# Per-image mixed 3x3 convolution on one core: pair 0's first weights summed on TensorE, pair 1's root on GpSimd, and loads from pair 8 on issued after the stores have landed

## What is computed

```python
pooled = x.mean(axis=(2, 3))                       # x: group-normalised input, 32 x 64 x 56 x 56, 32 groups
a = relu(pooled @ fc1_w.T + fc1_b)                 # K = 4 values per image
att = softmax(a @ fc2_w.T + fc2_b, axis=1)         # four mixing weights per image
agg_w = einsum('bk,koihw->boihw', att, weight)     # each image has its own 3x3 kernel
agg_b = att @ bias
out = x_raw + conv3x3(x, agg_w, pad 1) + agg_b     # x_raw: the input before the normalisation
```

## Time and profile before

| | us |
|---|---|
| median of 3 runs (304.75 to 305.0) | 304.8 |
| the profiled execution | 304.24 |
| its span, first to last instruction | 302.5 |
| TensorE busy | 297.2 (98% of the span) |
| VectorE, ScalarE, GpSimd busy | 245.9, 189.7, 17.7 |
| first product of pair 0 | 13.82 |
| granted TensorE clock, mean | 1.00 |

### The profile page before, as it was taken

How to read it: one execution, slowest core, us unless ns; L and a number is a source line. 1 busy time by engine, 2 the same in 40 slices (tenths; PEclk the granted TensorE clock), 3 DMA queues, 4 the chain that set the end, 5 groups by cost and what they waited for, 6 DMA issues and landing times.

```text
span 302.5 us, 15876 instructions
## 1 busy us (share of the span) xinstructions
PE 297.2 (98%) x7065; PEld 273.1 (90%) x7065; DVE 245.9 (81%) x799; ACT 189.7 (63%) x246; POOL 17.7 (6%) x30
## 2 busy tenths in 40 slices
PE   8999999999999999999999999999999999999995
PEld 6778997799978997799999999999999999999874
DVE  4898989989999999898998989699696978956000
ACT  3757739194674927385496868577585866768222
POOL 2231040403100000000000000000000000000000
PEclk9999999999999999999999999999999999999999
DMA  7857866647457583846708788765657242332333
GB/s 268 317 168 214 262 184 200 215 146 191 152 163 218 175 243 135 223 144 173 258 14 245 239 242 266 204 197 165 191 150 240 95 123 70 111 102 81 93 113 104
DMA packets 27012, 53.62 MB, mean 177 GB/s; under 512 B 6080, under 2 KB 16704, under 8 KB 26944
## 3 DMA queue, kind: packets, MB, share of 16 engines
q1 hardware_dynamic: 26720, 52.53, 57.6%
q10 hardware_dynamic: 224, 0.07, 0.1%
HBM read 26.89 MB, written 25.69 MB: 174 GB/s over the span
## 4 chain that ended last, share of the span: by engine, by line
PE 95%; DMA 3%; ACT 0%; POOL 0%; DVE 0%; issue 0%; DVEq 0%
PE acc L1068 94%; DMA w_sb<-w_t 1%; DMA x<-x 1%; ACT o L875 0%; PE acc L1048 0%; PE acc L1036 0%; PE tiny L1005 0%; POOL wnorms L418 0%; DVE o L792 0%; PE tiny L1022 0%; PE tiny L1026 0%; PE acc L1042 0%; DVEq L790 0%
## 5 line engine op out<-in xcount | busy, mean ns | idle before, releaser
L1068 PE MATMUL acc<-xh,wh 64*64 64x385 f16 (+5 forms) x2304 | 112.6, 325 | 0.0
L1068 PE MATMUL acc<-xh,wl 64*64 64x385 f16 (+5 forms) x2304 | 112.4, 325 | 0.0
L1068 PE MATMUL acc<-xl,wh 64*64 64x385 f16 (+5 forms) x2304 | 111.7, 325 | 0.0
L1068 PEld LDWEIGHTS acc<-xl,wh 64*64 64x64 f16 x2304 | 91.3, 107 | 6.0
L1068 PEld LDWEIGHTS acc<-xh,wl 64*64 64x64 f16 x2304 | 90.6, 107 | 6.8
L1068 PEld LDWEIGHTS acc<-xh,wh 64*64 64x64 f16 x2304 | 89.5, 107 | 7.2 <-ACT wh L864 0.3
L914 ACT ACTIVATE o<-acc,par 128x392 f32<-128x392 f32 (+1 forms) x64 | 42.9, 671 | 56.9 <-PE acc L1068 56.9
L458 DVE BATCH_NORM_STATS2 stats<-x 128x6 f32<-128x448 f32 x105 | 61.2, 617 | 1.8
L835 ACT ACTIVATE xh<-x,xof,xsc 128x1568 f16<-128x1568 f32 x24 | 40.5, 1689 | 25.1 <-DVE xof L545 24.6
L702 DVE TENSOR_TENSOR xl<-x,xh 128x1568 f16<-128x1568 f32 x28 | 49.8, 1783 | 3.3 <-ACT x L802 3.2
L593 DVE SCALAR_TENSOR_TENSOR mix<-w_sb,ex,mix 128x576 f32<-128x576 f32 (+1 forms) x69 | 42.8, 620 | 0.5
(11 more groups left out here) (106 smaller groups left out, 161.6 us busy)
## 6 DMA issues: line engine op xcount, KB each, us to landing
x<-x SPq DMA_DIRECT2D x60, 392.0 KB, 4.0
out<-o SPq DMA_DIRECT2D x36, 196.0 KB, 3.6
out<-o SPq DMA_DIRECT2D x72, 98.0 KB, 2.8
out<-o SPq DMA_DIRECT2D x8, 588.0 KB, 3.3
out<-o SPq DMA_DIRECT2D x16, 294.0 KB, 4.2
w_sb<-w_t SPq DMA_DIRECT2D x2, 576.0 KB, 4.1
x<-x SPq DMA_DIRECT2D x2, 448.0 KB, 4.2
out<-o SPq DMA_DIRECT2D x7, 112.0 KB, 2.2
```

The costliest lines, as they stand in the source:

```text
L1068: ins = nc.tensor.matmul(pixels[:, top:bottom, left:right], weights[i][halves[m], tap * C:(tap + 1) * C], window, start=start and step == ...
```

## The change

1. **Start of pair 0, TensorE.** All four shares of the three centre-row taps are summed on TensorE: the centre tap (64 columns) in `acc[2][1]` with the residual, the two side taps (128 columns) in `tiny[0]`. `part_mix` and VectorE's addition are gone. ScalarE reads both sums from PSUM (`first_high_weights`), and so does VectorE for the low part. The products begin with the centre tap of all three groups, then the side taps of all three, and then go on as before. `keep_warm` has 2 products after the range instead of 4, 3 and 3. The second product of the weights' norm is moved ahead of the semaphore `s_range`.
2. **Start of pair 0, VectorE and ScalarE.** VectorE makes four `diagonals`, then `wsc`, then two strips of xh that ScalarE made before (3 and 6); ScalarE has strip 7 alone left, later. `low_inputs(0, 0)` comes before the weights' bound and before all seven chunks of pair 1's statistics.
3. **Pair 1's root.** `second_group_stats` takes the root from GpSimd (`ALU.pow`), behind `second_low_inputs(0)` on its queue, in place of the Newton steps. The sums of pair 1 are asked for 2 steps into group 2's last kind and not 6; the first chunk of pair 2 moves behind the logits of pair 1.
4. **Pairs 8 to 11, SP.** Before each quarter of x, SP waits until the stores of this group have landed.

The core of the diff:

```diff
-WARM_PRODUCTS = (38, 6, 15, 4, 3, 3)
+WARM_PRODUCTS = (38, 6, 15, 2)
...
-SUMS_AT = ((1, 2, 6), (1, 2, 2), (1, 2, 2), (1, 1, 8), (1, 0, 8), (1, 0, 1), (0, 2, 6), (0, 2, 4), (1, 0, 2))
+SUMS_AT = ((1, 2, 2), (1, 2, 2), (1, 2, 2), (1, 1, 8), (1, 0, 8), (1, 0, 1), (0, 2, 6), (0, 2, 4), (1, 0, 2))
...
+        def first_piece(n, t):
+
+            return (t[:, CENTRE * C:(CENTRE + 1) * C], sides(t), t[:, PARTS[1]], t[:, PARTS[2]])[n]
+
+        def mixed_piece(n):
+
+            if n == 0:
+                return acc[SLOTS - 1][1][:, CENTRE_SUM]
+            if n == 1:
+                return tiny[0][:, SIDES_SUM].rearrange("p (t c) -> p t c", c=C)
+            return mix[:, PARTS[n - 1]]
...
                         cross_params(p + 1)
                     if p + X_RING < PAIRS:
+
+                        for r in range(2):
+                            sp.wait_ge(stored[p % 2][r], 16 * (1 + r) * (transfers(p) + g + 1))
                         load_quarter(p + X_RING, g)
...
+            second_low_inputs(0)
+            pool.wait_ge(s_mv, 2)
+            nc.gpsimd.tensor_tensor(rstd[:], mv[:, 1:2], minus_half[:], ALU.pow).then_inc(s_root, 1)
+            for p in range(1, EARLY):
                 second_low_inputs(p)
...
+                for k in range(K):
                     nc.vector.tensor_scalar(diagonals[:, k, :], eye[:], ex[:, k:k + 1], None, ALU.mult).then_inc(s_diagonal, 1)
+                    if k == 0:
+                        nc.vector.tensor_reduce(exsum[:], ex[:], AX.X, ALU.add).then_inc(s_exsum, 1)
+                for k in range(2):
+                    first_scale_step(k)
+                high_strip(6)
+                high_strip(3)
+                low_part(0)
+                dve.wait_ge(s_weights[0], 16)
...
             high_strip(4)
             first_mixture()
+            dve.wait_ge(s_scaled, 1)
+            low_inputs(0, 0)
             weights_bound()
             chunk_stats(1, 0, 1)
-            dve.wait_ge(s_scaled, 1)
-            low_inputs(0, 0)
             chunk_stats(1, 1, CHUNKS)
             exchange_stats(1)
-            group_stats(1)
+            second_group_stats()
             for p in range(1, EARLY):
                 logits(p)
+                if p == 1:
+
+                    chunk_stats(2, 0, 1)
                 mixture_in_parts(p)
...
             exponentials(0)
 
             first_high(5, 6, s_quarter[2])
-            first_high(2, 4, s_quarter[1])
-            high_weights_part(0, 0)
-            first_high(6, 8, s_quarter[3])
+            first_high(2, 3, s_quarter[1])
+            first_high_weights(0)
+            first_high_weights(1)
             first_share(2)
             first_high(0, 1, s_quarter[0])
-            high_weights_part(0, 1)
+            first_high_weights(2)
+            act.wait_ge(s_v_strip, 3)
+            first_high(7, 8, s_quarter[3])
 
             normalise_quarter(0, 1)
-            high_weights_part(0, 2)
+            first_high_weights(3)
             normalise_quarter(0, 2)
             normalise_quarter(0, 3)
...
+            def centre_share(k):
+
+                pe.wait_ge(s_weights[k // 2], 16)
+                pe.wait_ge(s_diagonal, k + 1)
+                for m in range(2):
+                    nc.tensor.matmul(acc[SLOTS - 1][1][halves[m], CENTRE_SUM], diagonals[halves[m], k, :],
+                                     first_piece(0, w_sb[:, k, :])[halves[m]], start=k == 0, stop=False)
+
+            def sides_share(k):
+
+                for m in range(2):
+                    ins = nc.tensor.matmul(tiny[0][halves[m], SIDES_SUM].rearrange("p (t c) -> p t c", c=C),
+                                           diagonals[halves[m], k, :], first_piece(1, w_sb[:, k, :])[halves[m]],
+                                           start=k == 0, stop=k == K - 1)
+                    if k == K - 1:
+                        ins.then_inc(s_sides_sum, 1)
+
+            def first_residual():
+
                 pe.wait_ge(s_eye, 1)
                 pe.wait_ge(s_eye_exsum, 1)
-                centre = slice(PART_SUM.start + C, PART_SUM.start + 2 * C)
                 for m in range(2):
-                    nc.tensor.matmul(acc[SLOTS - 1][1][halves[m], centre], eye_exsum[halves[m], :], eye_std[halves[m], :],
-                                     start=False, stop=True).then_inc(s_part_sum, 1)
+                    nc.tensor.matmul(acc[SLOTS - 1][1][halves[m], CENTRE_SUM], eye_exsum[halves[m], :],
+                                     eye_std[halves[m], :], start=False, stop=True).then_inc(s_centre_sum, 1)
...
             keep_warm(3)
-            part_sum()
-            weights_range()
-            keep_warm(4)
-
-            pe.wait_ge(s_part, 2)
-            keep_warm(5)
-
-
-            for n in range(len(PARTS)):
-                steps = range(3 * n, 3 * n + 3)
+
+            centre_share(0)
+            sides_share(0)
+            centre_share(1)
+            centre_share(2)
+            centre_share(3)
+            first_residual()
+            for k in range(1, K):
+                sides_share(k)
+
+
+
+            for n in range(2):
                 pe.wait_ge(s_wh, n + 1)
                 for g in range(SLOTS):
```

More of the change, by code:

```diff
@@ L422, in _ @@
             nc.gpsimd.tensor_scalar(eye_exsum[:], eye[:], exsum[:], None, ALU.mult).then_inc(s_eye_exsum, 1)
-            for p in range(EARLY):
+            second_low_inputs(0)
+            pool.wait_ge(s_mv, 2)
+            nc.gpsimd.tensor_tensor(rstd[:], mv[:, 1:2], minus_half[:], ALU.pow).then_inc(s_root, 1)
+            for p in range(1, EARLY):
                 second_low_inputs(p)
@@ L863, in high_weights_part, with first_high_weights @@
                 part = PARTS[n]
-                nc.scalar.activation(wh[i][:, part], mix[:, part], ACT.Copy, scale=wsc[i][:]).then_inc(s_wh, 1)
+                nc.scalar.activation(wh[i][:, part], mixed_part(p, n), ACT.Copy, scale=wsc[i][:]).then_inc(s_wh, 1)
+            def first_high_weights(n):
+                if n == 0:
+                    act.wait_ge(s_wsc, 1)
+                    act.wait_ge(s_centre_sum, 2)
+                elif n == 1:
+                    act.wait_ge(s_sides_sum, 2)
+                else:
+                    act.wait_ge(s_part, shares(0, n))
+                nc.scalar.activation(first_piece(n, wh[0]), mixed_piece(n), ACT.Copy, scale=wsc[0][:]).then_inc(s_wh, 1)
             def first_share(n):
@@ L1021, in first_range @@
                 pe.wait_ge(s_wnorms, 1)
-                nc.tensor.matmul(tiny[1][:, RANGE:RANGE + 1], scale[:], wnorms[:], start=False, stop=True).then_inc(s_range, 1)
-            def weights_range():
-                nc.tensor.matmul(tiny[0][:, WEIGHTS:WEIGHTS + 1], scale[:], wnorms[:],
-                                 start=True, stop=True).then_inc(s_weights_range, 1)
-            def part_sum():
-                part = PARTS[0]
-                pe.wait_ge(s_weights[0], 16)
-                for k in range(SUMMED_SHARES):
-                    pe.wait_ge(s_diagonal, k + 1)
-                    for m in range(2):
-                        nc.tensor.matmul(acc[SLOTS - 1][1][halves[m], PART_SUM], diagonals[halves[m], k, :], w_sb[halves[m], k, part],
-                                         start=k == 0, stop=False)
+                nc.tensor.matmul(tiny[1][:, RANGE:RANGE + 1], scale[:], wnorms[:], start=False, stop=True)
@@ new lines, in first_range @@
+                nc.tensor.matmul(tiny[1][:, WEIGHTS:WEIGHTS + 1], scale[:], wnorms[:],
+                                 start=True, stop=True).then_inc(s_range, 1)
+            def centre_share(k):
[4 more added lines that the diff above has]
+                                     first_piece(0, w_sb[:, k, :])[halves[m]], start=k == 0, stop=False)
@@ L1121, in _ @@
                     elif (n, g) == (0, 2):
-                        pe.wait_ge(s_quarter[3], 1)
-                    elif (n, g) == (1, 0):
-                        pe.wait_ge(s_quarter[0], 1)
-                    high(0, g, steps)
-                pe.wait_ge(s_wl, n + 1)
+                        pe.wait_ge(s_v_strip, 3)
+                        pe.wait_ge(s_wl, 1)
+                    high(0, g, (range(1), range(1, 3))[n])
+            for n in range(len(PARTS)):
+                steps = range(3 * n, 3 * n + 3)
+                if n > 0:
+                    pe.wait_ge(s_wh, n + 2)
+                    pe.wait_ge(*((s_quarter[0], 1) if n == 1 else (s_quarter[3], 1)))
+                    for g in range(SLOTS):
+                        high(0, g, steps)
+                pe.wait_ge(s_wl, n + 2)
                 for g in range(SLOTS):
```

83 lines of the change are left out of this document (47 added, 36 removed).

## The result

The changed kernel takes 315.99 us (median of 4 runs, 315.59 to 318.62) against 304.77 for the kernel before beside it (4 runs, 304.42 to 305.0): ratio 1.0389, 95% interval 1.0365 to 1.0413. It is 11.2 us slower; 3.5 were forecast. The four executions took 315.59, 315.64, 316.33 and 318.62 us at mean granted clocks of 0.998, 0.999, 0.995 and 0.988, so the two longer ones lost something to the clock as well. The profiled execution took 315.59, its span 313.8, against 304.24 and 302.5.

A forecast was written before the change was run, and what follows sets the result against it. TensorE's products bound the kernel, 94% of the chain: a 13.8 us start, 16 periods of 17.82 and an end. Profiled 304.24 - 0.3 (start) + 3.8 (SP's waits) = 307.7, median 0.56 above: 308.3 us, range 304.2 to 312.9.

The forecast's parts named there:

- The copy of pair 9: SP's queue: the second copy of par lands at 185.0 us, 5.9 after the load at 179.1; before it was 180.75.
- The slack of 4 us: Copies of par in the kernel before: they could land 4 us later before TensorE waits; 0.3 was forecast missing.
- the deadline of 184.7: Latest landing of the copy of par, 11.8 us of ScalarE and VectorE work ahead of TensorE's sums at 196.7.
- the law 13T - 58: Loss in us for SP's mean turn T in pairs 8 to 11: (T - 4.45) + 3 x (4T - 17.82).
- the turn: SP's queue, one load to the next, pairs 8 to 11: 4.75 us against TensorE's 4.455 a group; ends 4.3 to 6.2.
- rival 3: SP's turn is 5.5 us or more, as with foreign traffic; 13.7 us lost, 318 us; chance 0.07.
- The 4.6 of the earlier trace: Landing of a lower store with more traffic, 4.6 us, giving a turn of 6.2, the upper end.
- the upper store's issue: SP's turn of 5.1: issue took 1.13 us against 0.53, 0.6 put down to older traffic the wait removes.
- TensorE's holes: Four holes at the sums (L1067) of pairs 11 to 14, the last three about 1.2 us each.
- The start: Start of pair 0 through pair 1's sums: net -0.25, called -0.3 us; bounds -0.9 to +0.7.
- Ten products fewer cost nothing as long as the clock stays: Ten fewer products of ones on TensorE cost nothing; clock was granted at 1.00 with TensorE busy only 0.67.
- Rival 1: SP's turn fits under 4.455 us, so the waits lose nothing; 304.5 us; chance 0.30.

The follow-up runs named there:

- the kernel with two pairs: Changed kernel with SP's waits in pairs 8 and 9 alone: 307.08 us against 304.48 for the kernel before, 1.0086.
- every kernel of the table: Losses measured: changed kernel 11.2 us; kernel before with waits added 14.9; changed with loads of 8 pixels a row 1.7; changed with quarter of TensorE's instructions from pair 8, 4.9.
- the second: Kernel before with SP's two waits in pairs 8 to 11 added and nothing else: 319.40 us against 304.48, 1.0482.
- the kernel that waits for the upper store alone: Changed kernel, but SP waits for the upper store's landing and not the two lower ones: 309.56 us against 304.51 for the kernel before, 1.0166.
- the kernel without waits: Changed kernel without SP's waits, start and pair 1's root as changed: 304.68 us against 304.48 for the kernel before, 1.0005.
- the kernel with ScalarE's copies: Changed kernel, waits kept, ScalarE issuing the two copies of par from pair 8 on: 309.85 us against 304.48 for the kernel before, 1.0161.

## Why the prediction was right in direction and wrong in size

**What held.** Slower, by SP's waits, with the mechanism as told: the loads wait, the copies of `par` stand behind them, ScalarE's first lower results of pairs 9 to 12 wait, then pair statistics, then TensorE. The copy of pair 9 was put at 185.0 and let ScalarE go at 184.46. The slack of 4 us was right: at 184.46, a quarter of a microsecond ahead of the deadline of 184.7, ScalarE had a hole of 4.01 and TensorE none at the sums that hang on it; in the kernel with two pairs it was released at 185.01, 0.3 behind the deadline, and TensorE waited 0.20 there. The period of 17.82 and the law 13T - 58 give the loss within 0.8 us for every kernel of the table in which the copies are the path, if the fallen clock of the second is left to its own account. For the kernel that waits for the upper store alone it misses by 2 us, as told there.

**What failed: the turn.** "I take 4.75, between 4.4 and 5.1." It was 5.29, and 13 x 0.54 = 7.0 us of the 7.7 that the time lies above the forecast are this one term. It lies inside the band of 4.5 to 5.5 to which the prediction gave 0.55, but the range of times was drawn only to a turn of 5.1. Every step of it was issue plus landing from calm places: landings of 2.8 and 3.3. The turns without a fetch packet bear it out, 4.71 and 4.79 in the changed kernel. What was wrong is the sentence against rival 3, that "there is no traffic but its own". The page of the kernel before has this line:

```profile
q8 instruction: 55, 0.90, 1.2%
```

Its 1.2% of the engines' time looked like nothing, but a wait for a landing ends with the slowest of 16 engines, and 13 of 15 turns from load to load had such a packet. The 4.6 of the earlier trace rows was already one: in the kernel before the store issued at 190.71 met a fetch packet at 192.35 that ran 0.96 us. It was read as "more traffic" and put into the upper bound, when it was an event whose rate the trace gives: in the kernel before 14 packets between 178 and 250 us, in which TensorE ran 3,534 products and weight loads, so one for about 250 of them (12 for 3,084 in the changed kernel). The Trainium skill, Runtime: NRT & Kernel Launch, section Instruction fetch mechanics, says that an engine's instructions are refilled in blocks of 16 KiB, 256 instructions, over DMA, and that this is mostly hidden. The packets' size and their rate here agree; hidden it is from TensorE, not from who waits for a store.

**A step that was right for a wrong reason.** "Of this 0.6 is the upper store's issue, held up by older traffic which the wait removes." The wait did not remove it: in seven turns of the changed kernel the issue of a store took 1.1 to 2.3 us (as `195.02 1.58 SPq L332` in its chain) with all earlier stores landed and only the turn's own load under way; in six of them a fetch packet had begun 0.4 to 1.0 us after the load. These turns then landed 1.6 to 2.1 us behind the end of their last issue, where two calm others took 2.8, so in six of them the sum of both came out near the forecast, at 4.7 to 5.1; the one with the issue of 2.3 took 5.83.

**TensorE's holes** were forecast at the sums, 1.2 each. The sums had 2.6 us in three holes (longest 1.0), and 5.7 us more stood at products that waited for ScalarE's results (longest 2.4), since ScalarE, released late, also evicts late. Together with 0.7 at products that waited for VectorE's `xl` these are 9.0 of the 11.3 us; TensorE's busy time is also 2.1 longer (299.3 against 297.2), and no run says why. The forecast named one place for what is spread over two.

**The second path** was not in the prediction: loads of x that come late for the statistics of the last pairs. It costs 3 us alone in the times compared and nothing beside the first, so it didn't move the time; as a rival it was missing.

**The start.** Forecast -0.3; the trace shows -0.1 at 61.9 us, and the kernel without waits lies between -0.15 and +0.43. The first product was put at 13.21 and came at 13.48, as the weights' norm kept TensorE until 11.96, where the first share had been put at 11.73. In the profile of the kernel with two pairs, in which it didn't, shares began at 11.74 and the first product at 13.34. The side products, put at 13.9, began at 14.13, with their weights ready at 14.08. The lead of 0.34 us at the first product is 0.21 after the twelve products of the centre, two of whose steps took 0.22 and 0.24 us where a step takes 0.165, and 0.11 behind the sums of pair 1, a step of 0.22 at the sums included: all of it gain that I had counted. The wait for the sums was put at 0.2 and was 0.25. "Ten products fewer cost nothing as long as the clock stays" holds for the runs of the kernel without waits, whose mean clock was 0.998 to 1.00 in all eleven; it failed in the kernel with ScalarE's copies.

**Rival 1** (turn under 4.455, 0.30) has one turn of 13 for it, 4.43. The rule of the Trainium skill named there (DMA: Bandwidth & Descriptors, Anatomy of one DMA), an estimated 3.8 us for a load and its stores, has none: the shortest turn of 67 with load and three stores is 4.43.

## What to carry to other kernels

A wait for a transfer's landing ended here with the slowest of 16 DMA engines, so price it with a tail and not with a calm case: look at the packets of the instruction queue, since this unrolled stream of matmuls put one of about 1 us into 13 of 15 turns. When a wait is put into an in-order queue once a group, the question is its mean turn against the consumer's period; past break-even a tenth of a microsecond is paid for every turn that follows. Find all that queues behind it (here copies and loads) and the slack of each, because when the first path is cured the second one shows.

## What the runs showed of the hardware

- One 16 KB packet of the instruction queue on one DMA engine, 0.9 to 1.3 us long, went with a turn longer by 1.2 to 1.4 us when it began 3.0 to 4.1 us into it (6.10 against 4.69 to 4.94), and the last one to three of 48 parts landed 0.8 to 1.5 us behind the others. Packets that began in the first 3 us of a turn, beside the load, ran 0.9 to 2.5 us.
- A load of 392 KB ahead of three stores costs a turn about 1 us: 3.67 to 3.78 us without it, 4.7 to 4.8 with it.
- The granted clock fell to 0.50 behind one hole of 3.92 us, and in another kernel at 12.5 us behind two microseconds in which TensorE was busy for 0.64 and 0.42; it was back at 1.00 from 234.2 and 16.0 us. Each stretch at half speed was 3.4 us long, so it cost at most 1.7. Behind the profiled changed kernel's own holes, up to 2.4 us, it stayed at 1.00.
- At the very start TensorE's products of 256 columns stood 0.213 us apart and then 0.109, a factor of two like that between 1.2 and 2.4 GHz. The views print a clock of 1.00 throughout, but the trace has no record of the clock before this step, so that 1.00 isn't a reading. The step came at 5.3 us in the profiled execution of the changed kernel and anywhere from 4.2 to 7.2 us in the others. In the kernel without waits it came at 6.8, and pair 0's sums were 0.5 us late for it (10.55 against 10.07 before). So single executions differ at the start by more than the change was to gain there.
